# A graph-attention layer with a routed expert layer on one core: the router stage reordered

## The reference

```python
x = x + gnn(layernorm(x))        # six 1024x1024 projections with biases, 16 heads of masked
                                 # softmax attention over the graph's edges, output projection wo, bo
x = x + ffn(layernorm(x))
# ffn:
xf = layernorm(h) * ln_g + ln_b            # h = layernorm(x), mean and variance over 1024
logits = xf @ router_w                     # 8 experts
scores, idx = top_k(logits, 2); gate = softmax(scores)
# each expert: layernorm(xf)*eg + eb, x1 = .@W1+b1, x2 = clip(.@W2+b2, 20),
# hidden = x1 * x2 * sigmoid(x2), y = clip(hidden @ Wo + bo)
out = sum over experts of gate * y
```

## Time and profile before

| what | value |
|---|---|
| median of 3 runs | 579.73 us (577.4 to 579.78) |
| span of the profiled execution | 574.8 us |
| PE, PEld busy | 514.5, 444.6 us |
| DVE (VectorE) busy | 430.0 us |
| ACT (ScalarE), POOL (GpSimd) busy | 280.2, 234.6 us |
| mean granted TensorE clock | 0.954 |

### The profile page before, as it was taken

How to read it: one execution, slowest core, us unless ns; L and a number is a source line. 1 busy time by engine, 2 the same in 40 slices (tenths; PEclk the granted TensorE clock), 3 DMA queues, 4 the chain that set the end, 5 groups by cost and what they waited for, 6 DMA issues and landing times.

```text
span 574.8 us, 6831 instructions
## 1 busy us (share of the span) xinstructions
PE 514.5 (89%) x2579; PEld 444.6 (77%) x2579; DVE 430.0 (75%) x669; ACT 280.2 (49%) x406; POOL 234.6 (41%) x143
## 2 busy tenths in 40 slices
PE   3899999999999998989988886579999999996994
PEld 3899889999999997878877674456777676674773
DVE  6558977734433345889997776866999999997996
ACT  3425313332332235767775013329669659647630
POOL 5000433333333411122226712323686696690762
PEclk9999999999999999889999979569999999998889
DMA  8289763343344331020016233574888988984632
GB/s 315 94 282 343 234 260 121 121 146 98 125 147 146 128 137 70 1 74 1 1 58 210 114 111 109 196 285 175 328 322 310 388 313 324 391 298 180 220 110 111
DMA packets 20929, 106.32 MB, mean 185 GB/s; under 512 B 4720, under 2 KB 5104, under 8 KB 11168
## 3 DMA queue, kind: packets, MB, share of 16 engines
q1 hardware_dynamic: 15328, 91.53, 42.7%
q0 software_dynamic: 3696, 7.96, 4.2%
q10 hardware_dynamic: 1872, 6.39, 3.6%
HBM read 98.96 MB, written 6.91 MB: 184 GB/s over the span
## 4 chain that ended last, share of the span: by engine, by line
PE 52%; DVE 28%; issue 8%; ACT 5%; POOL 4%; DMA 1%; DVEq 0%; ACTq 0%; POOLq 0%
PE ps L1115 46%; DVE lo L728 11%; DVE sg L1031 4%; PE ps L1178 3%; POOL xres L480 2%; PE ps L1218 1%; ACT hi L561 1%; DVE xres L1047 1%; ACT xg L645 1%; DVE y L1001 1%; DVE hh L1038 1%; DVE x2c L1027 1%; DVE xg_lo L988 1%; DVE ht_lo L993 1%; ACT sg L654 1%
## 5 line engine op out<-in xcount | busy, mean ns | idle before, releaser
L728 DVE TENSOR_TENSOR lo<-raw,hi 128x2048 fp32r<-128x2048 f32 x58 | 153.8, 2668 | 54.8 <-ACT hi L561 54.6
L561 ACT ACTIVATE hi<-raw 128x2048 fp32r<-128x2048 f32 x70 | 131.8, 1913 | 77.0 <-PE ps L1115 65.0
L447 POOL DMA_INDIRECT mask_rows<-colf,bits x48 | 55.9, 1164 | 134.7 <-DMA mask_rows<-colf,bits 82.1
L489 POOL TENSOR_TENSOR lo<-raw,hi 128x2048 fp32r<-128x2048 f32 x12 | 64.9, 5408 | 50.5 <-ACT hi L561 50.4
L1115 PE MATMUL ps<-xt_hi,hi 128*128 128x384 f32 x192 | 65.2, 340 | 2.2 <-DVE xt_lo L744 2.2
L1115 PE MATMUL ps<-xt_lo,hi 128*128 128x384 f32 x192 | 65.1, 339 | 0.0
L1115 PE MATMUL ps<-xt_hi,lo 128*128 128x384 f32 x192 | 64.9, 338 | 0.0
L1115 PE MATMUL ps<-hi,xg_hi 128*128 128x512 f32 x128 | 54.3, 425 | 7.2 <-DVE lo L728 5.7
L1115 PE MATMUL ps<-lo,xg_hi 128*128 128x512 f32 x128 | 52.3, 409 | 0.0
L1115 PE MATMUL ps<-hi,xg_lo 128*128 128x512 f32 x128 | 52.2, 408 | 0.0
L455 POOL TENSOR_SCALAR pr<-pr,small 128x384 f32<-128x384 f32 x16 | 19.9, 1246 | 75.0 <-DVE small L853 75.0
(11 more groups left out here) (209 smaller groups left out, 1131.1 us busy)
## 6 DMA issues: line engine op xcount, KB each, us to landing
raw<-in_wf SPq DMA_DIRECT2D x42, 1024.0 KB, 6.3
raw<-in_wg SPq DMA_DIRECT2D x28, 1024.0 KB, 5.5
xfb<-in_wf SPq DMA_DIRECT2D x6, 1024.0 KB, 5.8
src_i<-in_srcb ACTq DMA_DIRECT2D x4, 768.0 KB, 6.2
dst_i<-in_dstb ACTq DMA_DIRECT2D x4, 768.0 KB, 9.0
y_rows<-y SPq DMA_DIRECT2D x6, 512.0 KB, 2.9
xin<-in_x SPq DMA_DIRECT2D x3, 512.0 KB, 4.4
xres<-in_x SPq DMA_DIRECT2D x3, 512.0 KB, 4.2
```

The source lines that it names most:

```text
L447: pool.indirect_dma_start(out=mbuf[:, :], out_offset=bass.IndirectOffsetOnAxis(ap=bits[:, 1, g:g + 1], axis=0), in_=colf[:, 5, g:g + 1], i ...
L489: pool.tensor_tensor(lo[SLOT[c]][:, :], raws[RAW[c]], f32(hi[SLOT[c]][:, :]), ALU.subtract).then_inc(pool_lo_done, 1)
L561: act.activation(hi[SLOT[c]][:, :], raws[RAW[c]], ACT.Copy).then_inc(hi_done, 1)
L728: dve.tensor_tensor(lo[SLOT[c]][:, :], raws[RAW[c]], f32(hi[SLOT[c]][:, :]), ALU.subtract).then_inc(lo_done, 1)
```

## The change

The output bias is loaded before the attention ends and added earlier (its first tile before the fill of `brow_f`); GpSimd's small constants move ahead of the heads. The router no longer multiplies xf: with u = (xres - mean) * g (`centre`, in halves), logits = (u @ W) * r + (b @ W), where b @ W (`bw`) is 8 more fp32 matmuls from a column layout of ln_b (`lnbc`). `router(t-1)` moves from k = 6 to k = 2. The final normalisation of z moves from VectorE (one operation) to ScalarE (scale and bias, from one more small product on GpSimd). The splits of chunks 29 and 30 on VectorE move one tile earlier, that of hi of chunk 32 on ScalarE too. The token list of expert 0 is copied and gathered alone. `keep_busy` adds fp32 matmuls of 128 columns whose result isn't used: 4 and 12 around router(2), 2 after each expert's sums but the first, 12 after the last. VectorE scales the second half of the first expert's tokens. `layouts` gains the input `lnbc`. Context lines are cut.

```diff
@@ -168,8 +168,8 @@
             lngb, lnbb = raw5[:, 0:D], raw5[:, D:2 * D]
-            x2c = sb(ffn, "x2c", [P, CW], F32)
-            sg = sb(ffn, "sg", [P, CW], F32)
+            x2sg = sb(ffn, "x2sg", [P, 2 * CW], F32)
+            x2c, sg, bob = x2sg[:, 0:CW], x2sg[:, CW:2 * CW], x2sg[:, 0:D]
@@ -189,7 +189,7 @@
             xfb = sb(ffn, "xfb", [P, NT + 1, D], F32)
-            xf, bob = xfb[:, 0:NT, :], xfb[:, NT, :]
+            xf, u = xfb[:, 0:NT, :], xfb[:, NT, :]
@@ -213,6 +213,7 @@
             over_cols = sb(ffn, "over_cols", [P, 2, KT], F32)
+            lnbc, bw = over_cols[:, 0, :], over_cols[:, 1, :]
@@ -306,6 +308,8 @@
         SUM_BANKS = [(0, 1), (5, 6), (2, 7)]
+        LOGITS = [B[0][:, 0:NE], B[0][:, NE:2 * NE], B[3][:, 4 * NE:5 * NE]]
+        TOK_BANK = [B[2], B[4]] + [B[7]] * (NE - 2)
@@ -360,16 +364,14 @@
                 sp.dma_start(xres[:, t, :], xv[:, t, :]).then_inc(resid_in, 16)
-            for a, b in ((lngb, lng), (lnbb, lnb)):
+            for a, b in ((bob, bo), (lngb, lng), (lnbb, lnb)):
                 sp.dma_start(a, b.partition_broadcast(P)).then_inc(resid_in, 16)
-            sp.wait_ge(o_ready, HEADS)
-            sp.dma_start(bob, bo.partition_broadcast(P)).then_inc(resid_in, 16)
+            for a, b in ((rws[:, :, :], rw), (lnbc, lnbc_in), (egb[:, 0, :, :], egc), (egb[:, 1, :, :], ebc)):
+                sp.dma_start(a, b).then_inc(ffn_in, 16)
...
                     sp.dma_start(brow_f[r:r + NE, cut], a).then_inc(ffn_in, 16)
-            for a, b in ((rws[:, :, :], rw), (egb[:, 0, :, :], egc), (egb[:, 1, :, :], ebc)):
-                sp.dma_start(a, b).then_inc(ffn_in, 16)
@@ -449,15 +451,6 @@
-            for h in range(HEADS):
-                pool.wait_ge(first_inverse, h + 1)
-                pool.tensor_scalar(pr[:, h % 2, 0, :], pr[:, h % 2, 0, :], rinv[:, h % 2, 0:1], None,
-                                   ALU.mult).then_inc(first_normalised, 1)
...
-            pool.wait_ge(o_ready, HEADS)
-            pool.memset(brow_f[:, :], 0.0).then_inc(rows_in, 1)
@@ -475,14 +468,28 @@
+            for h in range(HEADS):
+                pool.wait_ge(first_inverse, h + 1)
+                pool.tensor_scalar(pr[:, h % 2, 0, :], pr[:, h % 2, 0, :], rinv[:, h % 2, 0:1], None,
+                                   ALU.mult).then_inc(first_normalised, 1)
...
+            def add_bias(t):
+                pool.tensor_tensor(xres[:, t, :], xres[:, t, :], bob, ALU.add).then_inc(resid_ready, 1)
...
             pool.wait_ge(resid_in, 16 * 6)
+            add_bias(0)
+            pool.wait_ge(o_ready, HEADS)
+            pool.memset(brow_f[:, :], 0.0).then_inc(rows_in, 1)
+            for t in range(1, NT):
+                add_bias(t)
             for t in range(NT):
-                pool.tensor_tensor(xres[:, t, :], xres[:, t, :], bob, ALU.add).then_inc(resid_ready, 1)
-            for t in range(NT):
...
-                for n in range(2):
-                    pool.wait_ge(var_ready, 2 * t + n + 1)
-                    pool.tensor_tensor(fr[:, t, 4 + 2 * n:5 + 2 * n], fr[:, t, n:n + 1], halfneg, ALU.pow).then_inc(fr_ready, 1)
+                pool.wait_ge(var_ready, 2 * t + 1)
+                pool.tensor_tensor(fr[:, t, 4:5], fr[:, t, 0:1], halfneg, ALU.pow).then_inc(fr_ready, 1)
+                pool.wait_ge(var_ready, 2 * t + 2)
+                link(pool.tensor_tensor(fr[:, t, 6:7], fr[:, t, 1:2], halfneg, ALU.pow))
+                pool.tensor_tensor(fr[:, t, 5:6], fr[:, t, 3:4], fr[:, t, 6:7], ALU.mult).then_inc(fr_ready, 1)
@@ -505,10 +512,11 @@
             gather_tokens(0, 0)
+            pool.wait_ge(tok_ready, 2)
...
             select(1, 1)
-            pool.wait_ge(tok_ready, 2)
+            pool.wait_ge(tok_ready, 3)
@@ -631,7 +639,9 @@
                     act.activation(xft[:, 4 * a:4 * a + 4, :].rearrange("p k n -> p (k n)"), B[6 + a], ACT.Copy).then_inc(xft_ready, 1)
-                for c in ((29, 30), (31,), (32,))[t]:
+                act.wait_ge(fr_ready, 2 * t + 2)
+                act.activation(xf[:, t, :], xf[:, t, :], ACT.Identity, scale=fr[:, t, 6:7], bias=fr[:, t, 5:6]).then_inc(z_ready, 1)
+                for c in ((29, 30), (31, 32), ())[t]:
@@ -640,6 +650,11 @@
                 for a in range(2):
+                    if e == 0 and a == 1:
+                        act.wait_ge(dve_scaled, 1)
+                        act.sem_inc(xg_scaled, 1)
+                        act.activation(xg_hi[:, par, 4:8, :].rearrange("p k n -> p (k n)"), xg[:, par, CW:D], ACT.Copy).then_inc(xg_hi_done, 1)
+                        continue
@@ -878,11 +893,10 @@
-            dve.wait_ge(ffn_in, 16 * 9)
+            dve.wait_ge(ffn_in, 16 * 10)
...
             dve.wait_ge(rows_ready, 1)
-            dve.wait_ge(resid_ready, NT)
@@ -890,36 +904,47 @@
+            def centre(t, h):
...
+                cut = slice(h * CW, (h + 1) * CW)
+                dve.scalar_tensor_tensor(out=u[:, cut], in0=xres[:, t, cut], scalar=fmv[:, t, 0:1], in1=lngb[:, cut],
+                                         op0=ALU.subtract, op1=ALU.mult).then_inc(u_ready, 1)
...
+            def scale_logits(t):
...
+                link(dve.scalar_tensor_tensor(out=lg[:, t, :], in0=LOGITS[t], scalar=fr[:, t, 4:5], in1=bw,
+                                              op0=ALU.mult, op1=ALU.add))
...
             for t in range(NT):
+                dve.wait_ge(resid_ready, t + 1)
...
                     link(dve.tensor_tensor(xres[:, t, cut], xres[:, t, cut], B[2 * t + h], ALU.add))
-                    if h == 0:
-                        dve.bn_stats(xstat[:, t, h, :], xres[:, t, cut])
-                    else:
-                        link(dve.bn_stats(xstat[:, t, h, :], xres[:, t, cut]))
-                mean, v, a, b = fmv[:, t, 0:1], fmv[:, t, 1:2], fr[:, t, 2:3], fr[:, t, 0:1]
+                    link(dve.bn_stats(xstat[:, t, h, :], xres[:, t, cut]))
+                v, a, b = fmv[:, t, 1:2], fr[:, t, 2:3], fr[:, t, 0:1]
...
+                if t:
+                    dve.wait_ge(xf_turned, 2 * t)
+                centre(t, 0)
...
                 dve.tensor_tensor(b, a, v, ALU.add).then_inc(var_ready, 1)
-                link(dve.scalar_tensor_tensor(out=xf[:, t, :], in0=xres[:, t, :], scalar=mean, in1=lngb[:, :],
-                                              op0=ALU.subtract, op1=ALU.mult))
+                centre(t, 1)
+                dve.wait_ge(u_ready, 2 * t + 2)
                 dve.wait_ge(fr_ready, 2 * t + 1)
-                dve.scalar_tensor_tensor(out=xf[:, t, :], in0=xf[:, t, :], scalar=fr[:, t, 4:5], in1=lnbb[:, :],
-                                         op0=ALU.mult, op1=ALU.add).then_inc(xf_ready, 1)
...
-                dve.wait_ge(xf_ready, t + 1)
+                link(dve.scalar_tensor_tensor(out=xf[:, t, :], in0=u[:, :], scalar=fr[:, t, 4:5], in1=lnbb[:, :],
+                                              op0=ALU.mult, op1=ALU.add))
                 both_stats(xf[:, t, :], xstat[:, t, :, :], fmv[:, t, 2:4])
+                link(dve.tensor_scalar(fr[:, t, 3:4], fmv[:, t, 2:3], -1.0, None, ALU.mult))
                 dve.tensor_scalar(fr[:, t, 1:2], fmv[:, t, 3:4], EPS, None, ALU.add).then_inc(var_ready, 1)
-                if t > 0:
-                    split_lo(GNN_CHUNKS + t)
-                dve.wait_ge(fr_ready, 2 * t + 2)
-                dve.wait_ge(xf_turned, 2 * t + 2)
-                dve.tensor_scalar(xf[:, t, :], xf[:, t, :], fmv[:, t, 2:3], fr[:, t, 6:7], ALU.subtract, ALU.mult).then_inc(z_ready, 1)
...
+                if t < NT - 1:
+                    split_lo(GNN_CHUNKS + 1 + t)
...
+            dve.wait_ge(bw_ready, 1)
+            link(dve.tensor_copy(bw, B[2][:, NE:2 * NE]))
+            for t in range(NT - 1):
+                scale_logits(t)
@@ -936,7 +961,7 @@
             dve.wait_ge(logits_ready, NT)
-            link(dve.tensor_copy(lg, B[0][:, 0:NT * NE].rearrange("p (t e) -> p t e", t=NT)))
+            scale_logits(NT - 1)
@@ -952,9 +977,9 @@
                 ins.then_inc(slot_oh_ready, 1)
-                if e == 1:
-                    dve.wait_ge(tok_summed, 2)
-                    dve.tensor_copy(slot_tok[:, 0:2], B[2][:, 0:2]).then_inc(tok_ready, 1)
+                if e < 2:
+                    dve.wait_ge(tok_summed, e + 1)
+                    dve.tensor_copy(slot_tok[:, e:e + 1], TOK_BANK[e][:, e:e + 1]).then_inc(tok_ready, 1)
@@ -1001,6 +1026,11 @@
+            dve.wait_ge(xg_turned, 2)
+            for k in range(4, 8):
+                ins = dve.tensor_scalar(xg[:, 0, k * P:(k + 1) * P], B[6][:, (k % 4) * P:(k % 4 + 1) * P],
+                                        egb[:, 0, 0, k:k + 1], egb[:, 1, 0, k:k + 1], ALU.mult, ALU.add)
+            ins.then_inc(dve_scaled, 1)
@@ -1120,6 +1150,11 @@
+            def keep_busy(times):
...
+                for _ in range(times):
+                    pe.matmul(B[1][:, 0:P], ident[:, :], ident[:, :], start=True, stop=True)
@@ -1204,18 +1239,19 @@
             def router(t):
```

(34 more changed lines are left out.)

## The result

The changed kernel takes **587.15 us** (median of 4 runs, 586.41 to 590.25), the kernel before, on the same chip, 578.70 (4 runs, 577.4 to 579.78). The ratio is 1.0161, with a 95% interval of 1.0136 to 1.0185: 8.5 us slower, where the prediction gave 586.2 us and slower as the likeliest case.

What follows compares the result with a forecast made beforehand. VectorE, busy 57.7 of 60 us, bounds the expert loop, so any delay of its first clip passes on whole. X later by 9.3, tail shorter by 2.8, gather 0: +6.5 us, giving 586.2 us; range 578.5 to 590.5.

Steps and rivals of the forecast that it cites:

- Part 1: Earlier bias add and loads: VectorE idles from 315.2 to 318.9 us for bias rows, handing the gain to the late fill.
- S: Point where VectorE begins the residual of tile 0; forecast 325.1 us, between 322.5 and 327, before 325.3.
- Part 2: Router at the third step: TensorE stands 2.8 us at router(0), as before, and the clock is down until 338.0.
- X: Point where VectorE adds the last half tile of the projection; forecast 363.5 us, 9.3 later than 354.18.
- A: Rival: the clock stays at 2.4 GHz through both TensorE waits; 578.6 us, not slower; chance 0.13.
- B: Rival: Part 1 gains, S = 322.5, so the first TensorE wait is gone; 580.1 us; chance 0.17.
- both together: Rivals A and B combined: X = 353.5, 576.1 us, faster; chance 0.08.
- Part 3: Early split of chunk 29 makes VectorE wait for its buffer; TensorE stands 4.6 us at router(1), X 9.3 us later.
- Part 4: Tile 2 from X to L: 8.05 us where it was 10.86, a gain of 2.8.
- L: Point where the top-2 selection begins; forecast X + 8.05, before 365.04 us.
- Part 5: First expert's tokens: x2c at L + 22.9; gather hidden behind fillers, gain 0; sign: TensorE's own queue releases the first transposes.
- rival C: Fillers run at half clock, twelve of them taking 5.3 us; with both partly so 590 us; chance 0.12.

Runs made afterwards that it cites:

- e5: Changed kernel with the splits of chunks 29 and 30 back at the end of tiles 1 and 2 and the router back at the seventh step; 578.00 us.
- e1: Changed kernel with only the splits of chunks 29 and 30 back at the end of tiles 1 and 2; 583.53 us, ratio 1.0096.
- e2: Kernel before with only the splits of chunks 29 and 30 moved one tile earlier; 585.88 us, ratio 1.0130.
- e6: Changed kernel with only the router back at the seventh step, splits still early; 580.80 us, ratio 1.0039.
- e4: Changed kernel with the router stage's three weight loads issued ahead of the stores of z; 590.01 us, ratio 1.0205.
- e7: Changed kernel with router at the seventh step, split of chunk 29 at the end of tile 1, that of chunk 30 during the gather; 578.07 us.
- e3: Changed kernel without its filler matmuls; 584.62 us, ratio 1.0097.
- e10: e9 with ScalarE again scaling all of the first expert's tokens, as in the kernel before; 571.27 us, ratio 0.9870.
- e8: e7 without the filler matmuls; 573.99 us, ratio 0.9920.
- e11: Kernel before with only its router moved from the seventh to the third step; 583.50 us, ratio 1.0083.
- e9: e8 with the split of chunk 30 behind lo of the first expert's tokens; 572.36 us, ratio 0.9907.
- e12: e10 with the token lists of experts 0 and 1 copied together again, as before the change; 572.42 us, ratio 0.9882.

## Why the prediction was right

**Part 1** came out near the forecast by another way. S is 0.5 us earlier than predicted. The fill of `brow_f` ended at 317.04 less 2.94, that is 314.1 (forecast 315.1), but VectorE never stood idle for the rows as the prediction had it. In the timelines of GpSimd and VectorE, after:

```profile
312.88 2.42 POOL L479 TENSOR_TENSOR xres<-xres,x2sg 128x1024 f32<-128x1024 f32 x1 [6.83 <-DMA raw<-in_lnb]
315.24 1.80 POOL L484 MEMSET brow_f<- 48x2048 f32 x1
317.02 7.11 POOL L479 TENSOR_TENSOR xres<-xres,x2sg 128x1024 f32<-128x1024 f32 x2
```

```profile
313.60 8.26 DVE L743 TENSOR_TENSOR lo<-raw,hi 128x2048 fp32r<-128x2048 f32 x2 [1.32 <-ACT hi L569]
```

The first bias add took 2.42 us where I took 3.4; VectorE's two splits, beside it and what follows it on GpSimd, took 8.26 us, where two plain ones are 4.56. That the split would pay for the add wasn't in my working: the 3.7 us that I had given to the wait for the rows went there, and the sum hid it. That S came out so near was luck. Half of the 4.5 us that the GPSIMD Engine Reference of the Trainium skill (§ 3.1) gives for 2048 columns is an estimated 2.2 us for this add, which the 2.42 bear out. Its § 8 names contention with VectorE instructions that have two SBUF inputs, as these splits have; here the splits lost 3.7 us and GpSimd's two later adds 2.3 against the first.

**Part 2**: a wait of 2.35 us cost the clock, as taken; the half clock lasted to 340.5 us (337.5 less the shift), forecast 338.0. TensorE had stood as long in the kernel before, so the step held that this wait costs nothing new; it did not see that the new arithmetic could have saved it (X at O + 46.9 in e5, 54.3 in e1). Rivals A, B and both together are out: the clock fell at both waits, and S came too late to avoid the first.

**Part 3, the deciding step, held in each of its numbers**: VectorE idle for 11.63 us (from S + 9 to P + 1.95 is 11.5), TensorE for 4.71 (4.6), X later than before by 8.9 us from O (9.3). e2 shows the cause by itself, e1 shows it gone. Its price is less sure than its mechanism: undoing the splits gives back 3.6 us of the median (e1), undoing the early router 6.4 (e6).

**Part 4**: X to L took 7.99 us (8.05; before 10.86). z on ScalarE took 1.24 us; the 1.2 us estimated from ScalarE: Activation LUTs (Trainium skill, § What ACT_TABLE_LOAD costs) agrees. 

**Part 5 was right in its sum and wrong inside.** L to x2c took 24.0 us, forecast 22.9. Three terms were off. The fillers ended at L + 12.6 instead of 13.7. The gather took 7.41 us where 4.45 was taken from the earlier trace rows, landed at L + 12.8 instead of L + 9.9, and so it, 0.3 us behind TensorE's own queue, released the transposes: the sign that I named for this step failed in this execution and held in e1, e4, e5, e6 and e7. And the product took 7.39 us instead of 5.6: TensorE stood 2.21 us for the tokens' lo, the clock was at 0.50 again in 392 to 394 us, so "the fillers buy the clock and pay for it in full" failed in its first half: they kept the clock up for the transposes (1.09 us, in e3 1.97), but not for the product, which took 7.68 us without them (e3), hardly more. Fully warm it takes 5.82 (e5). The transposes began 0.8 us sooner than forecast, the tokens took 0.1 longer and the product 1.8: +1.1 us.

**The sum**: 7.2 us from O to x2c against 6.5 predicted; the medians differ by 8.5. The rest, 1.3 us, lies in executions that weren't profiled: rival C is a candidate, since e4 shows nearly the same code taking 3.5 us longer there, and one run of the changed kernel took 590.25. That the forecast of 586.2 is only 1.0 us under the measured time is in part luck: the difference was 2.0 us too small, and the base, 579.73 from three runs, was 1.0 above the 578.70 of four. And the 4.9 us between span and time are no constant: in every run that records both it is 1.7 to 1.9 (586.68 against 585.0), so the profiled execution of before, at 574.8, was some 2 us shorter than the median one. In the prediction's sum this cancels.

**Where the gain of the change went.** With the old order the new arithmetic brings X 5.4 to 6 us earlier in the profiles (e5, e10): u, scaled after the product, is ready when the router needs it, and neither the wait of 2.75 us at router(0) nor the half clock behind it is there. The median of e5 shows none of it (578.0 against 578.3); one reason is the fillers, which cost 4 us between e8 and e7. By the medians, the order of the splits costs 7.6 us (e2) and the early router 5.3 (e11), both with the old arithmetic, and the fillers 2.5 to 4 (e3, e8). With these three undone, the split of chunk 30 behind the tokens and ScalarE scaling them alone, it is 7 us faster than before (e10).

## What to carry to other kernels

Before you move a step forward in an in-order queue, look up when the buffer that it writes or reads comes free, by whom, and which short dependent chain stands behind it: a step that waits 11 us for its buffer costs what waits behind it, not its own 2 us. Independent work belongs behind the short chain that another engine waits for, not ahead of it. Filler work that is to hold a clock has to be priced at the lower clock and must not stand in front of the next real work. And undo one part of a change at a time: a change that loses as a whole can hold a gain.

## What the hardware showed that I had not expected

- The fillers' price grows by 1.7 when the clock is down: 24 passes of 128 columns took 2.92 us in the changed kernel and 5.06 in e7. They did bring the clock back (transposes and product of the first tokens 1.04 and 7.38 us in e7, 1.97 and 8.64 without fillers in e8), but for these 2.2 us the transposes began 7.1 us later behind L.
- A wait of 1.91 us ahead of router(1) was followed by half clock (e6). In e1, e5, e7, e8, e9, e10 and e12 the clock fell with no wait over 1 us close before, at 347.9 to 351.6 us: 0.2 to 1.2 us behind the passes of router(1), and in each of them before the passes of `bw` began. The same order of transposes and 16 passes at router(1) left the clock of the kernel before at 1.00 until 357 us. Why is open.
- Loads on their way lengthen the gather of the first tokens. Two loads of 1 MB were issued ahead of it; by how far, and how long the gather took: 3.7 us and 7.4 (after), 4.0 and 6.5 (e1), 4.7 and 5.7 (e6), 5.1 and 4.9 (e3), 5.7 or more and 4.4 to 4.6 (before and the other runs but e4). With one load alone, 4.7 us ahead, it took 4.5 (e4).
- GpSimd's elementwise work and VectorE's slow each other: two splits took 8.26 us instead of 4.56, while the add beside the first of them took 2.42 us and the next two 3.56 each. In the kernel before the second split ran beside the first bias add for 1.6 us and wasn't slowed (4.59 us for two); there the later subtraction on `brow` was, with 4.37 us instead of 2.28.
- Profiled executions differ by up to 3 us before the changed stage, with the granted clock between 222 and 240 us (0.91 or 0.72). Profiles of two kernels should be lined up at a common point before they are compared.
